# Two wide attention layers in double slots: two pairs of heads scored together, the two pairs ahead of them weighed right behind, and each turned weight matrix put over its own scores in PSUM

## The reference

```
# wide layer 1
normed = x * rsqrt(mean(square(x)) + 1e-6) * norm_w
q, k, v = heads(normed @ wq), heads(ctx @ wk), heads(ctx @ wv)     # (16, 16, S, 64)
attn = softmax(einsum('bhqd,bhkd->bhqk', q, k))
x = x + merge(einsum('bhqk,bhkd->bqhd', attn, v)) @ wo
# wide layer 2
q, k, v = rope(heads(x @ Wq)), rope(heads(ctx @ Wk)), heads(ctx @ Wv)
scores = where(mask, einsum('bhqd,bhkd->bhqk', q / 8, k), -1e9)
x = x + merge(einsum('bhqk,bhkd->bqhd', softmax(scores), v)) @ Wo
x = (x - mean) * rsqrt(var + 0.001) * ln_gamma + ln_beta
```

## Time and profile before

| what | value |
|---|---|
| time, median of 3 runs | 2113.66 us (2110.45 to 2115.55) |
| the profiled execution: its time, its span | 2111.77 us, 2109.8 us |
| TensorE busy (matmuls) | 1983.6 us, 94% |
| VectorE, ScalarE, GpSimd busy | 1414.2, 1276.3, 562.3 us |

### The profile page before, as it was taken

One profiled execution on the slowest core, in us unless ns is written; L12 is line 12 of the kernel. 1 busy time (PEld: TensorE's weight loads), 2 busy tenths in 40 slices (PEclk: granted clock), 3 DMA queues, 4 the chain that ended last, 5 costly groups with the idle time before them and its releaser, 6 DMA issues. The chain is left out here.

```text
span 2109.8 us, 50608 instructions
## 1 busy us (share of the span) xinstructions
PE 1983.6 (94%) x18664; PEld 1642.0 (78%) x18664; DVE 1414.2 (67%) x2898; ACT 1276.3 (60%) x3249; POOL 562.3 (27%) x676
## 2 busy tenths in 40 slices
PE   7999996978999999999999999999999998899997
PEld 6777775977888888888777787877878876777786
DVE  4777875544545545555577887888788874677775
ACT  3777775545555555555556665666566653677775
POOL 3323320000000000000035755766666651000000
PEclk8999998999999999999999999999999998899999
DMA  5434442021000000000001000000000001344442
GB/s 165 154 125 139 145 131 101 7 73 38 16 8 9 15 9 8 15 9 8 16 1 51 10 15 11 9 10 17 9 10 10 9 1 34 108 131 131 124 124 70
DMA packets 72858, 109.63 MB, mean 52 GB/s; under 512 B 7052, under 2 KB 62508, under 8 KB 72620
## 3 DMA queue, kind: packets, MB, share of 16 engines
q1 hardware_dynamic: 72332, 105.88, 16.5%
q10 hardware_dynamic: 288, 0.51, 0.1%
HBM read 69.18 MB, written 37.19 MB: 50 GB/s over the span
## 5 line engine op out<-in xcount | busy, mean ns | idle before, releaser
L1516 ACT ACTIVATE wide_P<-PS,MX 100x361 f32<-100x361 f32 x512 | 288.3, 563 | 407.3 <-DVE MX L1634 407.3
L1634 DVE TENSOR_REDUCE MX<-PS 100x2 f32<-100x722 f32 x256 | 231.7, 905 | 148.0 <-PE PS L1386 146.5
L615 ACT ACTIVATE L_P<-PS,MX 100x361 f32<-100x361 f32 x512 | 252.7, 565 | 122.0 <-DVE MX L745 122.0
L745 DVE TENSOR_REDUCE MX<-PS 100x2 f32<-100x722 f32 x256 | 219.6, 899 | 45.2 <-PE PS L501 44.9
L1815 POOL TENSOR_TENSOR wide_AC<-wide_T,wide_COSM 128x362 f32<-128x362 f32 x128 | 130.1, 1016 | 336.3 <-ACT wide_T L1465 334.1
L513 PE MATMUL PP<-CON,L_P 100*128 100x100 f32 x1536 | 184.1, 257 | 26.4 <-DVE L_PT L752 17.5
L513 PEld LDWEIGHTS PP<-CON,L_P 100*128 100x128 f32 x1536 | 151.2, 144 | 48.4 <-ACT L_P L615 33.7
L1395 PE MATMUL PP<-CON,wide_P 100*128 100x100 f32 x1536 | 176.5, 251 | 0.0
L1395 PEld LDWEIGHTS PP<-CON,wide_P 100*128 100x128 f32 x1536 | 161.1, 142 | 9.0 <-issue 2.3
L1409 PE MATMUL PS<-wide_PT,wide_V 128*64 128x100 f32 (+1 forms) x3072 | 161.9, 254 | 0.0
L1409 PEld LDWEIGHTS PS<-wide_PT,wide_V 128*64 128x64 f32 (+1 forms) x3072 | 136.8, 137 | 31.0 <-issue 23.3
(11 more groups left out here) (242 smaller groups left out, 5355.2 us busy)
## 6 DMA issues: line engine op xcount, KB each, us to landing
strips<-L_KS SPq DMA_DIRECT2D x256, 90.5 KB
L_KA<-strips SPq DMA_DIRECT2D x64, 362.0 KB, 3.1
C<-ctx_t SPq DMA_DIRECT2D x32, 361.0 KB, 3.1
kept<-L_CTH SPq DMA_DIRECT2D x16, 361.0 KB, 4.7
kept<-L_CTL SPq DMA_DIRECT2D x16, 361.0 KB, 5.5
L_CTH<-kept SPq DMA_DIRECT2D x16, 361.0 KB, 4.2
L_CTL<-kept SPq DMA_DIRECT2D x16, 361.0 KB, 5.0
C<-in_ctx SPq DMA_DIRECT2D x8, 256.0 KB, 3.4
```

What stands on the lines that cost most here:

```text
L615: nc.scalar.activation(P[:, (4 * g + j) % 8, 0:SK], PSB[0:SQ, j, 0:SK], ACT.Exp, bias=MX[:, s % 2, 4 * q + j:4 * q + j + 1], scale=1.0).th ...
L745: nc.vector.tensor_reduce(MX[:, s % 2, 4 * q + 2 * i:4 * q + 2 * i + 2], PSB[0:SQ, 2 * i:2 * i + 2, 0:SK], AX.X, ALU.max, negate=True).the ...
L1516: nc.scalar.activation(P[:, (2 * g + i) % 4, 0:SK], PS_[i][0:SQ, 0:SK], ACT.Exp, bias=MX[:, s % 2, h:h + 1], scale=1.0, accum_out=DEN[:, s ...
L1634: nc.vector.tensor_reduce(MX[:, s % 2, 2 * p:2 * p + 2], PSB[0:SQ, 0:2, 0:SK], AX.X, ALU.max, negate=True).then_inc(Z["maxed"], 1)
```

## The change

A slot now holds two pairs (G = 4s + d counts these double slots, d is 0 to 3), and `jobs_at` gives three lists: K jobs behind the weighing (first), others between the two turns (mid), Q and X at the end (late). TensorE runs the scores of 2G and 2G + 1, the weighing of 2G - 2 and 2G - 1, the first jobs, `turn(2G)`, the mid jobs, `turn(2G + 1)` and the late jobs. All four PSB banks hold scores (pair g in banks 2(g % 2) and the next), and the turned weights of a head go over its own scores; PP becomes the weighing's result and the third job bank. So scores wait for the unloads of g - 2 and no longer for the exponentials of g - 1, and a turn waits for its exponential alone. PT has four places in place of six. Both pieces of a context are split at the end of d = 1 (before: one each at the end of slots p = 2 and 3). The diff, cut to its core:

```diff
@@ -1141,8 +1141,8 @@
 
             NS, HP = 2 * B, H // 2
             NB, NT = 4, 3
-            BANKS = [*PJ, PSB[:, 3, :]]
-            PO = PSB[:, 2, :]
+            BANKS = [*PJ, PP[1]]
+            PO = PP[0]
             WK, WV, WQ = 0, 2048, 4096
...
-            PT = local("PT", [128, 6, KV_TILES * SQ])
+            PT = local("PT", [128, 4, KV_TILES * SQ])
...
-            def jobs_at(s, p):
-
-                after_scores, after_turn = [], []
+            def jobs_at(s, d):
+
+                first, mid, late = [], [], []
                 if s + 1 < NS:
-                    after_scores.append(("K", s + 1, p))
-                if s % 2 and s + 1 < NS:
-                    after_turn.append(("Q", s + 1, p))
-                if s % 2 == 0 and p == 7 and s + 2 < NS:
-                    after_turn.append(("X", s + 2, 0))
-                if p == 1 and s > 0:
-                    after_turn.append(("R", s - 1, 1))
-                if p == 5 and s > 0:
-                    after_turn.append(("O", s - 1, 0))
-                if p == 5 and s < NS:
-                    after_turn.append(("R", s, 0))
-                if p in (2, 3, 4) and s < NS:
-                    after_turn.append(("V", s, 3 + p - 2))
-                if p in (6, 7) and s + 1 < NS:
-                    after_turn.append(("V", s + 1, p - 6))
-                if p == 0 and 0 < s < NS:
-                    after_turn.append(("V", s, 2))
-                return after_scores, after_turn
-
-            SLOTS = [(s, p) for s in range(NS) for p in range(HP)] + [(NS, p) for p in range(6)]
+                    first += [("K", s + 1, 2 * d), ("K", s + 1, 2 * d + 1)]
+                    if s % 2:
+                        late += [("Q", s + 1, 2 * d), ("Q", s + 1, 2 * d + 1)]
+                if s % 2 == 0 and d == 3 and s + 2 < NS:
+                    late.append(("X", s + 2, 0))
+                if d == 0 and s > 0:
+                    mid.append(("R", s - 1, 1))
+                if d == 0 and 0 < s < NS:
+                    mid.append(("V", s, 2))
+                if d == 1 and s > 0:
+                    mid.append(("O", s - 1, 0))
+                if d == 2 and s < NS:
+                    mid.append(("R", s, 0))
+                if d < 3 and s < NS:
+                    mid.append(("V", s, 3 + d))
+                if d >= 2 and s + 1 < NS:
+                    mid.append(("V", s + 1, d - 2))
+                return first, mid, late
+
+            SLOTS = [(s, d) for s in range(NS) for d in range(4)] + [(NS, 0), (NS, 1)]
...
-            CHUNKS_AT = {(14, 2): [5], (14, 7): [6], (15, 0): [7], (15, 1): [8, 9], (15, 2): [10], (15, 6): [11]}
+            CHUNKS_AT = {(14, 1): [5], (14, 3): [6], (15, 0): [7], (15, 1): [8, 9], (15, 2): [10], (15, 3): [11]}
...
-            def turns_of(g):
-
-                if not 0 <= g < HP * NS:
+            def turns_of(G):
+
+                if not 0 <= G < 4 * NS:
                     return []
-                after_scores, after_turn = jobs_at(*divmod(g, HP))
-                return [key for key in after_scores + after_turn if key in turn_no]
+                first, mid, late = jobs_at(*divmod(G, 4))
+                return [key for key in first + late if key in turn_no]
+
+            def score_bank(g, i):
+                return PSB[:, 2 * (g % 2) + i, :]
...
-                        if g:
-                            pe.wait_ge(Z["exped"], 2 * g)
+                        if g >= 2:
+                            pe.wait_ge(Z["unloaded_even"], g - 1)
+                            pe.wait_ge(Z["unloaded_odd"], g - 1)
...
-                            if g:
-                                pe.wait_ge(Z[("unloaded_even", "unloaded_odd")[i]], g)
                             for t in range(KV_TILES):
-                                last = nc.tensor.transpose(PP[i][:, SQ * t:SQ * t + SQ], P[:, (2 * g + i) % 4, 128 * t:128 * t + 128], ident[0:SQ, 0:SQ])
+                                last = nc.tensor.transpose(score_bank(g, i)[:, SQ * t:SQ * t + SQ], P[:, (2 * g + i) % 4, 128 * t:128 * t + 128], ident[0:SQ, 0:SQ])
...
                         job(key)
-                    for s, p in SLOTS:
-                        after_scores, after_turn = jobs_at(s, p)
-                        g = HP * s + p
+                    for s, d in SLOTS:
+                        first, mid, late = jobs_at(s, d)
+                        G = 4 * s + d
                         if s < NS:
-                            scores(s, p)
-                        for key in after_scores:
+                            scores(s, 2 * d)
+                            scores(s, 2 * d + 1)
+                        if 1 <= G <= 4 * NS:
+                            weigh(2 * G - 2)
+                            weigh(2 * G - 1)
+                        for key in first:
                             job(key)
-                        if 1 <= g <= HP * NS:
-                            turn(g - 1)
-                        for key in after_turn:
+                        if s < NS:
+                            turn(2 * G)
+                        for key in mid:
                             job(key)
-                        if g % 2 and 3 <= g <= HP * NS + 1:
-                            weigh(g - 3)
-                            weigh(g - 2)
+                        if s < NS:
+                            turn(2 * G + 1)
+                        for key in late:
+                            job(key)
...
-                        if g >= 3:
-                            act.wait_ge(Z["weighed"], g - 2)
-                        nc.scalar.activation(PT[:, (2 * g + 1) % 6, :], PP[1][:, 0:KV_TILES * SQ], ACT.Copy).then_inc(Z["unloaded_odd"], 1)
+                        if g >= 2:
+                            act.wait_ge(Z["weighed"], g - 1)
+                        nc.scalar.activation(PT[:, (2 * g + 1) % 4, :], score_bank(g, 1)[:, 0:KV_TILES * SQ], ACT.Copy).then_inc(Z["unloaded_odd"], 1)
...
-                    for s, p in SLOTS:
-                        after_scores, after_turn = jobs_at(s, p)
-                        g = HP * s + p
+                    for s, d in SLOTS:
+                        first, mid, late = jobs_at(s, d)
+                        G = 4 * s + d
                         if s < NS:
-                            exponential(g, 0)
-                        for key in after_scores:
+                            for n in range(4):
+                                exponential(2 * G + n // 2, n % 2)
+                        for key in first:
+                            job(key)
+                        for key in turns_of(G - 1):
+                            rotated_high(key)
+                        if s < NS:
+                            unload(2 * G)
+                        for key in mid:
                             job(key)
                         if s < NS:
-                            exponential(g, 1)
-                        for key in turns_of(g - 1):
-                            rotated_high(key)
-                        if 1 <= g <= HP * NS:
-                            unload(g - 1)
-                        for key in after_turn:
+                            unload(2 * G + 1)
+                        for key in late:
                             job(key)
-                        if p in (2, 3) and s + 2 < NS:
-                            context_high(s + 2, p - 2)
-                        for c in CHUNKS_AT.get((s, p), ()):
+                        if d == 1 and s + 2 < NS:
+                            for k in range(KE):
+                                context_high(s + 2, k)
+                        for c in CHUNKS_AT.get((s, d), ()):
                             split_high(c)
...
-                    for s, p in SLOTS:
-                        after_scores, after_turn = jobs_at(s, p)
-                        g = HP * s + p
+                    for s, d in SLOTS:
+                        first, mid, late = jobs_at(s, d)
+                        G = 4 * s + d
                         if s < NS:
-                            maximum(g)
-                        shuffles_first = s + 1 < NS and rope(s + 1)
-                        if shuffles_first:
-                            for key in after_scores:
-                                job(key)
-                        if p == 2 and s:
+                            maximum(2 * G)
+                            maximum(2 * G + 1)
+                        for key in turns_of(G - 1):
+                            join(key)
+                        if d == 0 and s:
+                            invert(s - 1, 1)
+                        if d == 2 and s < NS:
+                            invert(s, 0)
+                        if d == 3 and s % 2 == 0 and s + 2 < B:
+                            x_norm(s + 2)
+                        for key in first:
+                            job(key)
+                        if s < NS:
+                            unload(2 * G)
+                        for key in turns_of(G - 1):
```

(45 more changed lines are left out.)

32 lines of the change are left out of this document (16 added, 16 removed).

## The result

| | before | after |
|---|---|---|
| time, median | 2114.11 us (2110.45 to 2115.55, 4 runs) | 2137.61 us (2133.89 to 2140.01, 4 runs) |
| span of the profiled execution | 2109.8 us | 2135.9 us |

The ratio is 1.0112, 95% interval 1.0093 to 1.0132: the change makes the kernel slower, by about 24 us. The forecast was 2085 us, and even its range (2050 to 2122) misses. One execution of the six-buffer kernel in the table further down took 5913 us and is left out of that kernel's median and ratio.

A forecast was written before the change was run, and what follows sets the result against it. In the wide layers the length of TensorE's stream and its stops were taken to bound the kernel. The terms -49 - 14 - 2 + 13 + 23 + 1 = -28 us against 2111.77 gave 2084, taken as 2085, range 2050 to 2122.

The forecast's parts named there:

- Borders (-49): TensorE, wide layers: fewer changes of tile shape save 0.38 us in each of 128 double slots, -49 us.
- Old waits (-14 and -2): Score products no longer wait for the previous exponential: -14 us, and -2 at the switch of weights between layers.
- New waits, first layer (+13): V waits at d=2 because both context pieces are split in a row: 14 sequences by 0.95 us, +13.
- cover of 0.3 us: First layer: the bank V needs was to be free 0.3 us before V comes, except at d=2.
- The unload's margin in double slots without queries: Second scores' unload hidden with 0.1 us to spare; if gone, 0.1 to 0.2 each, up to +7 in all.
- New waits, second layer (+23): Waits at d=2 and at the odd-to-even border: 2.9 us for two sequences, 8 times, +23 us.
- 1.2 us more: Second layer, odd-to-even border: the last rotated queries' join, due at 3.7 us, waits for GpSimd, losing 1.2 us.
- and about as much again: GpSimd's two products for queries: 0.71 us and about the same again, within 7.1 us for two keys and two queries.
- The switch of weights: Sequences 14 and 15: the large weight piece stands behind two context pieces, but the stall barely changes, +1 us.
- The rival of the ring: Odd second-layer sequences: four rotation buffers make GpSimd wait for keys' low half and set the pace; +58, 2143 us, chance 0.14.
- Borders not saved: TensorE's changes of tile shape save nothing and only waits are left over: 2135 us, slower, chance 0.05.
- hidden waits: ScalarE and VectorE run early enough to hide new waits, so only borders and old waits count: 2049 us, chance 0.20.

The follow-up runs named there:

- six-buffer kernel: The changed kernel with six buffers in place of four for rotated keys and queries; 2145.35 us, ratio 1.0159 to the kernel before.
- experiment with a key between: Changed kernel with query joins behind the shuffles and context pieces split apart, plus one key product between scores and weighing; 2106.91 us, ratio 0.9948.
- joins later: The changed kernel with VectorE's query joins moved behind the inverted denominators and the two shuffles; 2101.32 us, ratio 0.9940 to the kernel before.
- denominators first: The changed kernel with VectorE's inverted denominators ahead of all joins, shuffles still behind them; 2113.64 us, ratio 0.9994 to the kernel before.
- short joins: The changed kernel with VectorE's joins over 8 columns instead of 362 or 200; 2099.19 us, ratio 0.9907 to the kernel before.

## Why the prediction was wrong, point by point

- **Borders (-49): right.** 0.37 us a double slot in the first layer against 0.38, -47 in all; two sets of scores in a row pay nothing between them, the first key behind the weighing pays 0.11, both as assumed. The experiment with a key between gives the price once more.
- **Old waits (-14 and -2): right**, the row is gone.
- **New waits, first layer (+13): right in size, the mechanism in part.** 0.72 and 0.80 us a sequence in 16 sequences against 0.95 in 14, so +12. Only 0.44 of it comes from the two context pieces in a row, the place where the sum put all of it; 0.28 and 0.36 stay when they are apart, so the cover of 0.3 us in the sum wasn't there. That the total is near is luck in part: too much for the two pieces, nothing for the rest, and 14 sequences for 16. V at d=0 of odd sequences adds 0.17, about +1.
- **The unload's margin in double slots without queries (0.1 us, "up to +7"): gone**, as it was feared. 0.17 us three times in an even sequence, about +4 in the first layer; in the second 0.06.
- **New waits, second layer (+23): this is the step that failed.** "1.2 us more" at the border from an odd to an even sequence were 4.2 with three stops, plus 1.0 of half clock, the 1.2 of the odd d=2 were 1.8, the 0.5 of the even one 0.4, and stops of 1.3 at d=0 of the odd sequence were not in the sum at all: 8.7 us for two sequences in place of 2.9, or 70 us in place of 23. Two errors in it. First, the sum followed only when the last join is *due*; it did not follow what stands behind it in VectorE's order, R's input and two shuffles, so the one delay is paid at R and again at V (joins later: -36 us; denominators first: -24, with V's part left). Second, it took 0.71 us "and about as much again" from an average over a kernel in which the joins lay elsewhere; when joins run in a row, the product beside them takes 2.3 us (short joins: 0.61), and low halves of queries beside a product take three times their length (1.12 for 0.36). That is also what makes the second scores wait for an unload.
- **The switch of weights (+1, beside the -2 of the old wait there)**: sequences 14 and 15 are 2.0 us shorter together, borders and new waits included; small either way.
- **The rival of the ring: wrong in mechanism**, though its sign and its 2143 look close to 2137.61. Its wait is in the list (99.2 us), but it was the odd sequences that it would have lengthened, by 7 us each; they grew by 1.3, and the even ones by 2.7. Without that wait (six buffers) the kernel is slower.
- "Borders not saved" and "hidden waits" are both refuted by the account above.
- **The start of the phase (not in the sum)**: 5.6 us shorter, most of it a wait for a piece of context that fell from 5.4 to 0.9 us.
- **The chances** don't quite add up as written: the forecast and the rivals give 0.75 for faster and 0.19 for slower, where the summary has 0.77 and 0.17.

Put together for the wide phase: -47 for borders, -16 for old waits, +12, +4 and +1 in the first layer, +70 in the second, and -5 at the start: +19, measured +15.7; the remaining 3 us are not placed. The 9.5 us of the last narrow layer are scatter of two single executions; the medians differ by 23.5. What of that difference lies outside the wide phase in the other runs I can't say, since each kernel has one profile.

## What to carry to other kernels

Merging slots to save borders also merges the small work of the other engines into longer runs, and in an in-order program everything behind a run inherits its lateness: before costing such a change, write down for each engine what stands behind the last item of each run, and who waits for it. Put what TensorE waits for (here R's input and the shuffles that free a bank) ahead of work that is only due a slot later. And don't delete the largest wait of the list because it is large: GpSimd's 99 us cost nothing, and without them its products met VectorE's work more often.

## What the runs showed of the hardware

- A VectorE add or subtract of two SBUF operands and a GpSimd product hold each other up when they meet, and one side pays for both: GpSimd's 200-column product took 0.54 to 0.79 us at the border shown with no join beside it and 2.07 to 2.44 beside two or three joins, which kept their 0.53 and 0.36 us; it ended 0.48 us behind the last of them. VectorE's 200-column subtract took 0.36 and up to 1.14 us, its 362-column one 0.54 and, with six buffers, 1.24 in the median.
- After a double slot with some 4.3 us of TensorE lost in three stops its granted clock fell to 1.2 GHz for 3.4 us in five of eight places, 1.6 us each. The stops don't tell which: behind 1.4, 2.2 and 0.75 us it fell in sequence 24 and stayed at 2.4 GHz in sequence 28. Why there and not here stays open.
- Scores to weighing costs 0.12 us, weighing to keys 0.11, keys to weighing 0.09, and two sets of scores in a row nothing.
